# TensorE's row in a scan step: the sum of y two tiles back placed between the two pieces of the next tile's turned product

## The chip, the cores and the metric

The kernel runs on one core of one Trainium2 chip. The metric is device time in microseconds. A core has five engines that run their own instruction rows and meet only through semaphores: TensorE (PE in the profile), VectorE (DVE), ScalarE (ACT), GpSimd (POOL) and SyncE (SP), which issues the transfers. An engine takes its row in order: a wait at one instruction holds everything behind it.

## What is computed

Two images `b` of 1024 tokens with 128 channels go through a block with two residual branches. The first branch is a two-directional Mamba layer, the second a mixture of experts. The costly part is the recurrence of the Mamba layer, for each image and direction:

```python
xc = silu(conv(xh))                     # 256 channels
dbc = xc @ x_proj.T                     # dt, B (16), C (16) per token
delta = softplus(dt @ dt_w.T + dt_b)
def step(h, inp):
    u_t, d_t, B_t, C_t = inp
    h = h * exp(d_t[:, :, None] * A) + (d_t * u_t)[:, :, None] * B_t[:, None, :]
    return (h, einsum('bds,bs->bd', h, C_t))
y = (ys + xc * Dsk) * silu(z)
out = y @ out_proj.T
```

## The kernel before, in words

The loop over `e` runs 128 tiles. A *unit* `u` is one image and direction (4 units of 32 tiles; the second direction scans backwards), and within a unit the tile `t = e % 32` is one of 16 states for one half (128) of the channels. Each tile is 128 channels by 1024 tokens, and passes through four engines:

- ScalarE makes the decay `dA` (L605) and, one block of 128 tokens at a time, scales the input `dBuT`, tokens on partitions, with B (L621).
- TensorE turns `dBuT` into PSUM with channels on partitions, in two pieces of 512 tokens, `dbu_chunk(e + 1, 0)` and `dbu_chunk(e + 1, 1)`, four transposes each, into three banks `dBu0` to `dBu2`. Below they are c0 and c1. A piece waits until the scan three pieces back has freed its bank: in step `e`, c0 waits for both scans of tile `e - 1`, c1 for the first scan of tile `e`.
- VectorE scans the tile in two pieces (L1044 forward, L1047 backward).
- GpSimd multiplies the states by the row of C into `hc` (L519), three buffers deep.
- TensorE turns `hc` back and adds it onto `yT` in PSUM, eight transposes: `y_add(e - 2)`, the sum of y two tiles back, below y(e-2). It waits for that tile's product.

Between these, TensorE's row carries *items*, small pieces of the projections of the next unit and of the end of the last one: kinds X, Z, B, BT, DT, DU for the next unit (X takes two steps, the others one), YT and O for the last unit, and LT, LG and more in the last unit. All items of the loop share one PSUM bank, `pro`. So an item starts only after the item before it has been read out: by ScalarE in its own order (tanh L571 for X and Z, copies for the others) and for X and Z then by VectorE (L920, L924), which does this between the two scans of a tile. So a late item holds the second scan, too.

In steps `t` = 2 and 3 of a unit, TensorE starts `yT` anew with `y_start` (L1260 `yT<-dskip,area`), once VectorE has closed the last unit's half with a gate (L1055). The gate of a half stands on VectorE between the scans of tile `t` = 1 (half 0) or 2 (half 1) and waits for the last y of that half, which TensorE adds in step `t` = 0 or 1.

The four tiles of `DIRECT` (tiles 40, 41 and 72, 73) have their product made by GpSimd (L495), not TensorE: the steps 39, 40, 71 and 72 turn no piece.

The lines L1260 and L1264 are the helpers through which every matmul and transpose go; the tiles' names tell them apart: `dBu<-ident,dBuT` is c0 and c1, `yT<-ident,hc` is a sum of y, `pro<-...` is an item.

Of the kernel before, what the change touches and what calls it, by code (L numbers as in the profile page):

```python
# [138 lines left out]
def build_block(nc, x_d, mod_d, wpack_d, bcast_d, dtw_d, w1_d, w2_d, crow_d, out_d):  # L139
# [5 lines left out]
    with ctx:  # L145
# [188 lines left out]
        def chunks(u):  # L334

            return range(NCH) if u % 2 == 0 else range(NCH - 1, -1, -1)
# [118 lines left out]
        def _(g_):  # L455
# [25 lines left out]
            def pool_du(half, u):  # L481
                _, _, par = unit(u)
                wait_delta(g_, half, u)
                for c in range(NCH):
                    wait_item(g_, "X", half * NCH + c, u)
                g_.tensor_tensor(du[:, half, :], delta[par][:, half, :], xc[par][:, half, :],
                                 ALU.mult).then_inc(du_ready, 1)
# [45 lines left out]
        def _(act):  # L533
# [57 lines left out]
            def softplus(u):  # L591
                _, _, par = unit(u)
                wait_item(act, "DT", NH * NCH - 1, u)
                for half in range(NH):
                    nc.scalar.activation(delta[par][:, half, :], pre[:, half, :], ACT.Softplus).then_inc(delta_ready, 1)  # L595

            def exp_tile(e):

                u, s, half = e // (DS * NH), e // NH % DS, e % NH
                _, dr, par = unit(u)  # L600
                if s == 0:
                    wait_delta(act, half, u)
                if e >= 3:
                    act.wait_ge(scan_done, NCH * (e - 2))
                nc.scalar.activation(dA[:, e % 3, :], delta[par][:, half, :], ACT.Exp,  # L605
                                     scale=Aneg[:, dr, half, s:s + 1]).then_inc(da_ready, 1)
# [651 lines left out]
        def _(pe):  # L1258
# [3 lines left out]
            def turn(out, in_, start, idn=None):  # L1262

                return nc.tensor.matmul(out, in_, ident[:, :] if idn is None else idn, start=start, stop=True,  # L1264
                                        is_transpose=True, skip_group_check=True)
# [139 lines left out]
            def dbu_chunk(e, i):  # L1405

                u, half = e // (DS * NH), e % NH
                g, q = e // NH, NCH * e + i
                c = chunks(u)[i]
                if e == 0 and i == 1:  # L1410
                    pe.wait_ge(high0_ready, 1)
                elif half == 0:
                    pe.wait_ge(dbut_ready, max(NCH * SCALED.index(g) - 1, 0) + i + 1)
                if q >= 3:
                    pe.wait_ge(scan_done, q - 2)
                for k in range(BPC):
                    last = turn(dBu[q % 3][:, k * P:(k + 1) * P],
                                dBuT[:, SCALED.index(g) % 2, c * BPC + k, half * P:(half + 1) * P], True)
                last.then_inc(dbu_ready, 1)

            def y_start(u, half):

                _, dr, par = unit(u)
                if u > 0:
                    pe.wait_ge(gate_done, NH * (u - 1) + half + 1)
                for n in range(NBLK):
                    mm(yT[:, half, n, :], xc[par][:, half, n * P:(n + 1) * P], dskip[:, dr, half, :],
                       n % BPC == 0, True)

            def y_add(e):  # L1430

                half = e % NH
                if e == NT - 1:
                    pe.wait_ge(last_hc, 1)
                else:
                    pe.wait_ge(hc_done, e + 1)
                for n in range(NBLK):
                    last = turn(yT[:, half, n, :], hc[:, e % 3, n * P:(n + 1) * P], False)
                last.then_inc(yacc_done, 1)
# [18 lines left out]
            for e in range(NT):  # L1458
                u, t = divmod(e, DS * NH)
                for i in range(NCH):  # L1460
                    if e + 1 < NT and (e + 1) // NH not in DIRECT:
                        dbu_chunk(e + 1, i)
                for p in PARTS[e]:
                    item_t(*p)
                if t in (2, 3):
                    y_start(u, t - 2)
                if e >= 2:
                    y_add(e - 2)
            def gather(b, ns):

# [174 lines left out]
```

## Time and profile before

| | |
|---|---|
| median of 3 runs | 593.84 us (593.1 to 595.65) |
| the profiled execution's own time | 595.13 us |
| span of its profile | 593.3 us |
| mean granted TensorE clock | 0.945 |
| busy, share of the span | PE 84%, DVE 79%, ACT 74%, POOL 57% |

### The profile page before, as it was taken

To read this page: it belongs to the slowest core of one execution; us is meant where nothing else is said; L and a number is where in the kernel's file an instruction comes from. 1 tells how busy PE (TensorE), PEld (TensorE's weight loads), DVE (VectorE), ACT (ScalarE), POOL (GpSimd) and SP (SyncE) were. 2 spreads that over 40 slices of the span, in tenths; PEclk is the share of its full clock that TensorE was granted. 3 is DMA by queue.
4 is the path that set the end of the run, shared out by engine and by line. 5 is a ranking of instruction groups with operands and counts; after the bars stand their busy time and mean duration, and the time that the engine had idled before them with its cause. 6 is when DMAs were issued, how large, how long until landed. Compare 5 with 4: busy or idle time off the path is not lost.

```text
span 593.3 us, 9187 instructions
## 1 busy us (share of the span) xinstructions
PE 495.7 (84%) x3346; PEld 406.6 (69%) x3346; DVE 465.8 (79%) x709; ACT 439.6 (74%) x835; POOL 339.2 (57%) x159
## 2 busy tenths in 40 slices
PE   3578979996899999698998896788967486999997
PEld 2345856875779677576955676688855375698696
DVE  5856887976988787698899876988999999866422
ACT  2459875999996989999686799987879671374250
POOL 3104655867969777697895767857667573200000
PEclk9988997998999999899999897979989999978999
DMA  8031121221332222123222211312272214000101
GB/s 257 0 115 37 62 81 36 78 78 60 116 107 72 107 72 89 53 81 134 82 72 65 72 76 38 116 67 76 72 215 91 82 42 142 1 1 2 35 1 36
DMA packets 18237, 44.77 MB, mean 75 GB/s; under 512 B 1360, under 2 KB 7632, under 8 KB 17936
## 3 DMA queue, kind: packets, MB, share of 16 engines
q1 hardware_dynamic: 18192, 44.18, 22.3%
q8 instruction: 27, 0.44, 0.3%
q14 instruction: 18, 0.15, 0.1%
HBM read 42.61 MB, written 1.57 MB: 74 GB/s over the span
## 4 chain that ended last, share of the span: by engine, by line
PE 41%; ACT 26%; DVE 23%; issue 7%; POOL 1%; DMA 1%; POOLq 0%; DVEq 0%; ACTq 0%
ACT dBuT L621 12%; PE pro L1260 10%; DVE area L1047 9%; PE yT L1264 9%; PE yT L1260 9%; ACT dA L605 7%; PE dBu L1264 7%; PE dBu L1260 5%; DVE area L1044 3%; PE pro L1264 2%; DVE area L827 1%; ACT th L571 1%; ACT pre L580 1%; DVE pre L1009 1%; ACT area L595 1%
## 5 line engine op out<-in xcount | busy, mean ns | idle before, releaser
L519 POOL TENSOR_TENSOR hc<-area 128x1024 f32<-128x1024 f32 x127 | 302.7, 2389 | 148.1 <-DVE area L1044 87.6
L621 ACT ACTIVATE dBuT<-area,bT 128x256 f32<-128x256 f32 x492 | 208.4, 499 | 8.1 <-PE dBu L1264 8.1
L1264 PE MATMUL dBu<-ident,dBuT 128*128 128x128 f32 x992 | 143.3, 282 | 43.9 <-DVE area L1047 23.5
L605 ACT ACTIVATE dA<-area,Aneg 128x1024 f32<-128x1024 f32 x124 | 141.8, 1144 | 20.3 <-DVE area L1047 13.5
L1264 PEld LDWEIGHTS dBu<-ident,dBuT 128*128 128x128 f32 x992 | 115.1, 145 | 57.5 <-issue 21.2
L1264 PE MATMUL yT<-ident,hc 128*128 128x128 f32 x1024 | 140.7, 283 | 1.7 <-POOL hc L519 1.4
L1264 PEld LDWEIGHTS yT<-ident,hc 128*128 128x128 f32 x1024 | 120.8, 145 | 20.9 <-issue 15.4
L1047 DVE TENSOR_TENSOR_SCAN area<-dA,area,dBu 128x512 f32<-128x512 f32 x62 | 79.2, 1278 | 4.5
L1044 DVE TENSOR_TENSOR_SCAN area<-dA,area,dBu 128x512 f32<-128x512 f32 x62 | 79.2, 1277 | 4.1
L1044 DVE TENSOR_TENSOR_SCAN area<-dA,dBu 128x512 f32<-128x512 f32 x62 | 74.7, 1205 | 9.3 <-PE dBu L1264 8.7
L1047 DVE TENSOR_TENSOR_SCAN area<-dA,dBu 128x512 f32<-128x512 f32 x62 | 74.6, 1204 | 6.0 <-PE dBu L1264 5.5
L1260 PE MATMUL pro<-hT,wtap 128*128 128x512 f32 x96 | 48.2, 627 | 0.2 <-DVE area L924 0.2
L1260 PE MATMUL pro<-wp,hT 128*128 128x256 f32 (+1 forms) x96 | 23.2, 371 | 14.2 <-DVE area L924 12.6
L924 DVE SCALAR_TENSOR_TENSOR area<-th,pro 128x512 f32<-128x512 f32 x16 | 11.0, 687 | 25.4 <-ACT th L571 24.9
L571 ACT ACTIVATE th<-pro 128x512 f32<-128x512 f32 x28 | 16.4, 587 | 15.7 <-PE pro L1260 15.7
L1260 PEld LDWEIGHTS pro<-wp,hT 128*128 128x128 f32 x96 | 15.6, 201 | 18.1 <-DVE area L924 14.6
L1260 PEld LDWEIGHTS pro<-hT,wtap 128*128 128x128 f32 x96 | 17.3, 201 | 13.5 <-issue 12.6
L589 ACT ACTIVATE area<-pro 128x512 f32<-128x512 f32 x14 | 8.3, 591 | 16.9 <-PE pro L1264 16.9
L696 ACT ACTIVATE hc<-dBu,modT 128x512 f32<-128x512 f32 x2 | 1.6, 778 | 25.7 <-PE dBu L1260 25.7
L725 ACT ACTIVATE hc<-yT,wp 128x64 f32<-128x64 f32 x64 | 14.0, 330 | 8.5 <-PE yT L1260 8.5
L1260 PE MATMUL pro<-area,wp 128*96 128x512 f32 x28 | 14.9, 652 | 6.1 <-DVE area L837 6.1
L1260 PE MATMUL yT<-hc,dBuT 128*128 128x64 f32 x128 | 18.0, 302 | 0.0
(235 smaller groups left out, 598.5 us busy)
## 6 DMA issues: line engine op xcount, KB each, us to landing
area<-bc_rows SPq DMA_DIRECT2D x64, 512.0 KB, 3.6
dBuT<-w_in SPq DMA_DIRECT2D x1, 2048.0 KB, 9.1
wp<-wpack_in SPq DMA_DIRECT2D x1, 1030.0 KB, 7.3
x<-x_in SPq DMA_DIRECT2D x2, 512.0 KB, 6.6
hc<-bcast_in SPq DMA_DIRECT2D x1, 1024.0 KB, 10.5
Bb<-bc_rows SPq DMA_DIRECT2D x2, 512.0 KB, 3.9
out<-x SPq DMA_DIRECT2D x4, 256.0 KB, 2.3
bc_rows<-xdbl SPq DMA_DIRECT2D x4, 128.0 KB, 3.8
```

The source lines that it names most:

```text
L519: g_.tensor_tensor(hc[:, e % 3, :], hs[:, e % 3, :], Cb[:, g % 3, :], ALU.mult).then_inc(hc_done, 1)
L571: nc.scalar.activation(th[:, :], src, ACT.Tanh).then_inc(tanh_ready, 1)
L580: nc.scalar.activation(dst[:, half, c * CH:(c + 1) * CH], src, func, bias=dtb(dr, half)).then_inc(item_act, 1)
L589: nc.scalar.activation(yg[:, half, c * CH:(c + 1) * CH], src, ACT.Copy).then_inc(item_act, 1)
L605: nc.scalar.activation(dA[:, e % 3, :], delta[par][:, half, :], ACT.Exp, scale=Aneg[:, dr, half, s:s + 1]).then_inc(da_ready, 1)
L621: return nc.scalar.activation(dBuT[:, SCALED.index(g) % 2, n, :], duT[par][:, n, :], ACT.Copy, scale=bT[:, par, n, s:s + 1])
L725: last = nc.scalar.activation(hid[:, q % 2, i, c, :], up_bank(q)[:, at:at + TOPK], ACT.Gelu_apprx_tanh, bias=b1c[:, 2 * q + i, c:c + 1])
L924: nc.vector.scalar_tensor_tensor(gz[par][:, 2 * j:2 * j + 2, :].rearrange("p n d -> p (n d)"), th[:, :], 1.0, src, ALU.add, ALU.mult).then ...
L1044: nc.vector.tensor_tensor_scan(hs[:, e % 3, lo:hi], decay, inflow, init, ALU.mult, ALU.add).then_inc(scan_done, 1)
L1047: nc.vector.tensor_tensor_scan(hs[:, e % 3, lo:hi][:, ::-1], decay[:, ::-1], inflow[:, ::-1], init, ALU.mult, ALU.add).then_inc(scan_done, 1)
L1260: return nc.tensor.matmul(out, lhsT, rhs, start=start, stop=stop, skip_group_check=True)
L1264: return nc.tensor.matmul(out, in_, ident[:, :] if idn is None else idn, start=start, stop=True, is_transpose=True, skip_group_check=True)
```

## The change

In a step, TensorE's row was c0, c1, items, y. It becomes c0, y, c1, items. In the steps `t` = 2 and 3 nothing moves, since y must follow `y_start` there. In the steps without pieces (before the direct tiles) y now stands ahead of the items. Nothing is added or removed, and no other engine's row changes.

```diff
                 for i in range(NCH):
                     if e + 1 < NT and (e + 1) // NH not in DIRECT:
                         dbu_chunk(e + 1, i)
+                    if i == 0 and e >= 2 and t not in (2, 3):
+                        y_add(e - 2)
                 for p in PARTS[e]:
                     item_t(*p)
                 if t in (2, 3):
                     y_start(u, t - 2)
-                if e >= 2:
                     y_add(e - 2)
```

The first place is TensorE's row in the first unit, from `y_start` of step 3 to the item of step 5. The items here are of kind Z (`pro<-wp,hT`). Before:

```order
L1260 MATMUL yT<-dskip,area1 128x128 x8
L1264 MATMUL yT<-ident,hc 128x128 x8
L1264 MATMUL dBu1<-ident,dBuT 128x128 x4
L1264 MATMUL dBu2<-ident,dBuT 128x128 x4
L1260 MATMUL pro<-wp,hT 128x256 x2
L1264 MATMUL yT<-ident,hc 128x128 x8
L1264 MATMUL dBu0<-ident,dBuT 128x128 x4
L1264 MATMUL dBu1<-ident,dBuT 128x128 x4
L1260 MATMUL pro<-wp,hT 128x256 x2
```

With the change:

```order
L1260 MATMUL yT<-dskip,area1 128x128 x8
L1264 MATMUL yT<-ident,hc 128x128 x8
L1264 MATMUL dBu1<-ident,dBuT 128x128 x4
L1264 MATMUL yT<-ident,hc 128x128 x8
L1264 MATMUL dBu2<-ident,dBuT 128x128 x4
L1260 MATMUL pro<-wp,hT 128x256 x2
L1264 MATMUL dBu0<-ident,dBuT 128x128 x4
L1264 MATMUL yT<-ident,hc 128x128 x8
L1264 MATMUL dBu1<-ident,dBuT 128x128 x4
L1260 MATMUL pro<-wp,hT 128x256 x2
```

The first Z item of the fence has two sums of y between `y_start` and itself, where it had one; from there on there is one y between two items, as before.

The second place is TensorE's row around the direct tiles 40 and 41, from the last O item (its last two rows stand here) to the second half of the X item. Before:

```order
L1264 MATMUL pro<-ident,hT 128x128
L1260 MATMUL pro<-wp,area3 128x128 x2
L1264 MATMUL yT<-ident,hc 128x128 x8
L1260 MATMUL pro<-hT,wtap 128x512 x2
L1264 MATMUL yT<-ident,hc 128x128 x8
L1264 MATMUL dBu0<-ident,dBuT 128x128 x4
L1264 MATMUL dBu1<-ident,dBuT 128x128 x4
L1260 MATMUL pro<-hT,wtap 128x512 x2
```

With the change:

```order
L1264 MATMUL pro<-ident,hT 128x128
L1260 MATMUL pro<-wp,area3 128x128 x2
L1264 MATMUL yT<-ident,hc 128x128 x8
L1260 MATMUL pro<-hT,wtap 128x512 x2
L1264 MATMUL dBu0<-ident,dBuT 128x128 x4
L1264 MATMUL yT<-ident,hc 128x128 x8
L1264 MATMUL dBu1<-ident,dBuT 128x128 x4
L1260 MATMUL pro<-hT,wtap 128x512 x2
```

The sum between the O item and the X item was y(37), and y(38) followed the X item's first half; with the change y(37) stands ahead of this O item, and the sum between O and X is y(38).

The third place is TensorE's row at the start of the last unit, from c0 of tile 97 to `y_start`; the items `pro<-ident,pre` are LT. Before:

```order
L1264 MATMUL dBu2<-ident,dBuT 128x128 x4
L1264 MATMUL dBu0<-ident,dBuT 128x128 x4
L1264 MATMUL pro<-ident,pre 128x128 x4
L1264 MATMUL yT<-ident,hc 128x128 x8
L1264 MATMUL dBu1<-ident,dBuT 128x128 x4
L1264 MATMUL dBu2<-ident,dBuT 128x128 x4
L1264 MATMUL pro<-ident,pre 128x128 x4
L1264 MATMUL yT<-ident,hc 128x128 x8
L1264 MATMUL dBu0<-ident,dBuT 128x128 x4
L1264 MATMUL dBu1<-ident,dBuT 128x128 x4
L1260 MATMUL yT<-dskip,area1 128x128 x8
```

With the change:

```order
L1264 MATMUL dBu2<-ident,dBuT 128x128 x4
L1264 MATMUL yT<-ident,hc 128x128 x8
L1264 MATMUL dBu0<-ident,dBuT 128x128 x4
L1264 MATMUL pro<-ident,pre 128x128 x4
L1264 MATMUL dBu1<-ident,dBuT 128x128 x4
L1264 MATMUL yT<-ident,hc 128x128 x8
L1264 MATMUL dBu2<-ident,dBuT 128x128 x4
L1264 MATMUL pro<-ident,pre 128x128 x4
L1264 MATMUL dBu0<-ident,dBuT 128x128 x4
L1264 MATMUL dBu1<-ident,dBuT 128x128 x4
L1260 MATMUL yT<-dskip,area1 128x128 x8
```

The two sums, y(94) and y(95), for which the gates wait, have moved ahead of c1 and of the LT item of their step.

## Rows read from the trace of the kernel before

**Rows 1.** The page: engines' busy time, and the chain that ended last.

```profile
PE 495.7 (84%) x3346; PEld 406.6 (69%) x3346; DVE 465.8 (79%) x709; ACT 439.6 (74%) x835; POOL 339.2 (57%) x159
...
PE 41%; ACT 26%; DVE 23%; issue 7%; POOL 1%; DMA 1%; POOLq 0%; DVEq 0%; ACTq 0%
```

**Rows 2.** The page's costliest groups: the pieces and the sums of y on TensorE.

```profile
L1264 PE MATMUL dBu<-ident,dBuT 128*128 128x128 f32 x992 | 143.3, 282 | 43.9 <-DVE area L1047 23.5
...
L1264 PE MATMUL yT<-ident,hc 128*128 128x128 f32 x1024 | 140.7, 283 | 1.7 <-POOL hc L519 1.4
```

**Rows 3.** Waits of TensorE, 85 to 485 us: total, times, longest.

```profile
PE dBu L1264 <- DVE area L1047: 22.1, 23, 3.4
PE dBu L1264 <- DVE area L1044: 14.5, 11, 4.6
PE pro L1260 <- DVE area L924: 12.6, 6, 4.8
```

**Rows 4.** Busy time by stretch: length, PE, PEld, DVE, ACT, POOL, clock, DMA.

```profile
171.00:217.00 46.00, 45.71 (x314) 36.21 (x315) 37.17 (x34) 37.56 (x71) 36.52 (x16) 1.00 0.27 93
400.00:485.00 85.00, 63.38 (x509) 56.61 (x508) 79.94 (x119) 68.88 (x131) 58.50 (x26) 0.96 0.32 102
```

**Rows 5.** Timeline, first unit, step 4: TensorE, and ScalarE's tanh.

```profile
66.39 1.04 PE L1264 MATMUL yT<-ident,hc 128*128 128x128 f32 x8
67.26 1.04 PE L1264 MATMUL dBu<-ident,dBuT 128*128 128x128 f32 x8
...
66.90 0.57 ACT L571 ACTIVATE th<-pro 128x512 f32<-128x512 f32 x1
```

**Rows 6.** Timeline, second unit: its start, and the last ScalarE wait before 240 us.

```profile
169.81 0.57 ACT L571 ACTIVATE th<-pro 128x512 f32<-128x512 f32 x1
...
170.56 0.68 DVE L920 SCALAR_TENSOR_TENSOR area<-th,pro 128x512 f32<-128x512 f32 x1
...
171.29 0.66 PE L1264 MATMUL pro<-ident,area 128*128 128x128 f32 x4 [1.04 <-DVE area L920]
...
217.73 0.59 ACT L575 ACTIVATE xdbl<-pro 96x512 f32<-96x512 f32 x1 [0.24 <-PE pro L1260]
```

**Rows 7.** Timeline, direct tiles 40 and 41: TensorE's sums y(37), y(38); GpSimd.

```profile
189.10 1.04 PE L1264 MATMUL yT<-ident,hc 128*128 128x128 f32 x8
...
191.87 1.03 PE L1264 MATMUL yT<-ident,hc 128*128 128x128 f32 x8
...
184.15 4.69 POOL L495 TENSOR_TENSOR dA<-pre,Bb 128x1024 f32<-128x1024 f32 x2
188.79 7.02 POOL L519 TENSOR_TENSOR hc<-area 128x1024 f32<-128x1024 f32 x3
```

**Rows 8.** Timeline, direct tiles 72 and 73: item X, y(70), y(71); GpSimd; VectorE.

```profile
296.92 1.99 PE L1260 MATMUL pro<-hT,wtap 128*128 128x512 f32 x4
298.87 1.09 PE L1264 MATMUL yT<-ident,hc 128*128 128x128 f32 x8
...
303.59 1.09 PE L1264 MATMUL yT<-ident,hc 128*128 128x128 f32 x8
...
296.45 6.99 POOL L519 TENSOR_TENSOR hc<-area 128x1024 f32<-128x1024 f32 x3
...
304.53 0.66 DVE L920 SCALAR_TENSOR_TENSOR area<-th,pro 128x512 f32<-128x512 f32 x1
```

**Rows 9.** Timeline, start of the last unit: c1 of tile 96, y(94), the gate.

```profile
386.93 1.09 PE L1264 MATMUL dBu<-ident,dBuT 128*128 128x128 f32 x4 [4.57 <-DVE area L1044]
...
392.07 1.05 PE L1264 MATMUL yT<-ident,hc 128*128 128x128 f32 x8
...
393.16 1.23 DVE L1055 TENSOR_TENSOR area<-yT,area 128x1024 f32<-128x1024 f32 x1 [1.24 <-PE yT L1264]
```

**Rows 10.** Timeline, ScalarE after the softplus of two units.

```profile
143.02 1.31 ACT L621 ACTIVATE dBuT<-area,bT 128x256 f32<-128x256 f32 x3 [0.26 <-PE dBu L1264]
...
249.58 1.71 ACT L621 ACTIVATE dBuT<-area,bT 128x256 f32<-128x256 f32 x4 [0.28 <-PE dBu L1264]
```

## The prediction

> **What bounds the kernel now.** I read the page first. TensorE is the busiest engine, 84% of the span, but the chain that ended last gives it 41%, ScalarE 26% and VectorE 23% [rows 1]: the bound changes hands. The table of costly groups gives what the change is about. The 992 rows of the pieces stood behind 43.9 us of idle TensorE, most of it waiting for scans; the 1024 rows of the sums of y behind 1.7 us [rows 2]. So TensorE often stands at a piece while a sum that is ready lies behind it. The waits from 85 to 485 us say it again: 22.1 and 14.5 us at pieces for scans, 12.6 us at items for the readout of `pro` [rows 3]. Where does that idle time lie? From 171 to 217 us TensorE is busy 45.71 of 46 us; from 400 to 485 us VectorE is busy 79.94 of 85 and TensorE only 63.38 [rows 4]. So TensorE sets the time of the front of a unit, where it hardly waits, and waits where VectorE, or ScalarE around the softplus, sets the time. Filling idle time in the second kind gives nothing by itself. What counts is what the new order does to three things that others wait for: the items, the gates, the first pieces.
>
> **One sum costs 0.87 us of TensorE's row**: from the start of y at 66.39 to the start of the next piece at 67.26 [rows 5]. The count of transposes is unchanged, so in a saturated stretch the row's length is unchanged. What changes is which sum has been done when an item ends. Before, y(e-3) is done at the end of the item of step e; after, y(e-2). Between two items stand one sum and two pieces in both orders, so a saturated row neither gains nor loses from item to item. The shift is paid once per unit, at t = 4, the first step in which y moves ahead, since two sums then stand between `y_start` and the item. Each item from there is up to 0.87 us later, until TensorE has an idle gap at a piece that swallows the extra sum. Being one sum ahead is of no use to anyone unless somebody waits for a sum or for c0.
>
> **First unit, +0.4.** Item Z of step 4 ended at 66.39, where y began; now at 67.26. ScalarE was not free for its tanh until 66.90 [rows 5], so the lateness that gets through is 67.26 - 66.90 = 0.36 us, say 0.4. Bounds: 0 if a later slack eats it, 0.87 if ScalarE itself is early. ScalarE, the item's next user on VectorE and the second scan all hang on it, so it stays in the chain.
>
> **Second unit, +2.0 and -0.16.** At its start the X item's tanh is not held by TensorE but by ScalarE's own order, ending at 169.81 + 0.57 = 170.38; VectorE read the item at 170.56, behind a gate, and TensorE's next item, 1.04 us idle, followed at 171.29 [rows 6]. An earlier gate therefore gains 170.56 - 170.40 = 0.16 us, no more. From there TensorE is saturated [rows 4] to the handover at 217.73, where ScalarE waits for an item for the last time (0.24 us) [rows 6] and then sets the pace through the softplus. So the 0.87 us of t = 4 come through whole. On top comes the direct place. GpSimd makes two products for tiles 40 and 41 from 184.15 and only then product 38, which ends at 188.79 + 7.02/3 = 191.13 [rows 7]. Before, y(38) began at 191.87, after the X item, and waited for nothing. Now it stands ahead of the X item. The O item ahead of it ended at 189.10, where y(37) began [rows 7]; now, one sum later, at 189.97. TensorE then stands 191.13 - 189.97 = 1.16 us. What is queued behind: half an X item, the pieces of tile 42, the rest of X; VectorE's scans of 42 wait for them. In a saturated stretch nothing gives it back. Sum 0.87 + 1.16 = 2.0, bounds 0.9 (GpSimd early enough) and 3.2 (a whole product of 2.34 us waited for).
>
> **Third unit, +1.6 and -0.16.** Again 0.87 us at t = 4. Product 70 ends at 296.45 + 6.99/3 = 298.78; before, TensorE spent the time until then on the X item, from 296.92, and y(70) followed at 298.87 without loss [rows 8]. Now the X item (1.95 us) stands behind y(70). From y(70) to y(71) took 303.59 - 298.87 = 4.72 us [rows 8], of which about 0.75 was the wait of a piece that now passes beside the moved work; with X and one more sum ahead, the second half of X ends at 298.87 + 3.97 + 1.95 + 0.87 = 305.66, 2.1 us later than 303.59. ScalarE's tanh takes 0.6 us, so VectorE reads it at 306.3 where it did at 304.53 [rows 8]: +1.8 at most. Some of this meets norms on VectorE which end later anyway; I take 1.6, bounds 0.9 and 2.0. VectorE sets the time from here to 333 us and keeps it. The start gives 0.16 as in the second unit.
>
> **Last unit, -1.1.** This is where a sum is waited for. The gate of half 0 stood 1.24 us idle until y(94), begun at 392.07, was done [rows 9]. In the new row y(93) falls into TensorE's 4.57 us of waiting before c1 of tile 96 [rows 9], and y(94) follows c0 of tile 97, ahead of c1 and LT. It is then done by about 391, before VectorE has ended its scan at 391.92 (393.16 less the idle 1.24). So nearly all of 1.24 is gained; I keep 0.1 for the hop: -1.1. ScalarE is well ahead here, and VectorE carries the gain to the end. Bounds 0 and 1.3. The 0.87 us of t = 4 cost nothing where VectorE is the bound [rows 4].
>
> **After each softplus, -0.26 to -0.28, three times.** ScalarE waited 0.26 and 0.28 us for c0 [rows 10], because TensorE had been stuck at an item with y undone. With y done ahead, c0 follows the item at once, and ScalarE, which sets the pace there, gains it: -0.8 in all. Bounds 0 and 0.9.
>
> **The sum.** 0.4 + 2.0 + 1.6 - 0.32 - 1.1 - 0.8 = +1.8 us. Against the profiled execution's own 595.13 us this is 596.9; that execution lies 1.3 us above the median of the runs, so against the median 593.84 it is 595.6 us, 0.3% slower, inside the 0.5% (3 us) that a measurement of this kernel can tell from no change.
>
> **A rule weighed.** The rows show 36.6 us of TensorE waiting at pieces [rows 3] while only 1.7 us stood before sums [rows 2]; the case for a gain is that such time can be filled. The Trainium skill, Perfetto Trace Analysis, Optimization Strategies, says that in general the matmul engine should be kept as highly utilized as possible; by that rule the filled gaps would count as gain, which is the first rival below. The rows of 400 to 485 us speak against it here, with VectorE at 94%.
>
> **Rivals.** *Faster, the idle time is cashed.* For it: 36.6 us is nine times the losses that I count (4.0), and c0 goes to VectorE 0.87 us earlier in every step. Against it: where VectorE waited for c0, c1 comes no earlier, and the items hold the second scan. If one in ten of the waited microseconds came back and the items cost nothing, that and the gains at the starts make -3.7 - 0.3 - 1.1 = -5.1: 588.7 us.
> *Slower, GpSimd's queue.* The same two direct places, deeper: TensorE's late items delay the scans, so GpSimd's three-product tail starts later, and y(38) and y(70) each wait for a whole product, 2.34 us, in place of the 1.16 and about 0.9 counted. With what then follows once more at y(39) and y(71), +2.5 to +3: 598.4 us. It decides once product 38 ends more than 1.2 us later against TensorE's arrival than I have it.
> *Nothing arrives.* ScalarE's and VectorE's own queues eat the late items, the gains being as small: 593.8 us. For it: ScalarE was the later one in the first unit, by 0.5 us.
> *The clock.* With pieces and sums alternating, TensorE might idle for moments at every change of tile, and the grant fall in the saturated stretch, which ran at 1.00 with a change at every 0.4 to 2 us [rows 4]. At 0.94 as over the kernel, 46 us of work in each of three such fronts would be 2.8 us longer, +8 in all: 602 us. The Trainium skill, TensorE: Matmul & The Clock Gate, A second HAM failure mode, tells of a kernel in which cycling through PSUM banks did this. The 1.00 of this stretch does not bear it out.
>
> **Chances.** The forecast, +0.2 to +3.4 us with the bounds above: 0.52, of which 0.05 beyond 3 us. Nothing arrives: 0.12. Slower by GpSimd: 0.19. The clock: 0.02. Faster: 0.15. So faster 0.15, same 0.59, slower 0.26. The likeliest case's own range is 594.0 to 597.4. For 8 in 10 I go down to 591.3, into the faster case, and up to 599.3, above the GpSimd case.
>
> **What would show it.** Right: item Z of step 4 ends about 0.9 us later after `y_start`; TensorE stands 1 us or more at y(38) for L519, and 2 us at y(70), where the wait of sums in all was 1.7 us; the gate at the last unit's start shows no wait for TensorE; c0's wait of ScalarE after the softplus is gone; TensorE's waits at pieces shrink by tens of microseconds with the span unmoved. Wrong: if VectorE's busy share in 171 to 217 us rises, early c0 does speed the front, and I have missed who set it.

## The result: 596.95 us, 0.5% slower

| | before | changed |
|---|---|---|
| median of 11 runs each | 594.21 us (592.62 to 595.65) | 596.95 us (591.7 to 600.07) |
| ratio, 95% interval | | 1.0052 (1.0030 to 1.0074) |
| profiled execution: own time, span | 595.13, 593.3 us | 598.08, 596.4 us |
| mean granted TensorE clock | 0.945 | 0.937 |

The change costs 0.3 to 0.7%, 1.8 to 4.4 us. The ratios here and below leave out single executions more than 1.5% above the fastest of the same kernel: 954.15 us of a2_fronts_old, 602.13 of b2_softplus_only, 598.34 of b4_fronts_old_step10, 598.2 of c1_no_last and 818.77 of the kernel before.

The page of the changed kernel, its engines, the chain that ended last, and the two groups of [rows 1, 2]:

```profile
PE 499.5 (84%) x3346; PEld 410.4 (69%) x3346; DVE 465.5 (78%) x709; ACT 440.2 (74%) x835; POOL 340.4 (57%) x159
...
PE 36%; ACT 26%; DVE 25%; issue 8%; POOL 3%; DMA 1%; POOLq 0%; DVEq 0%; ACTq 0%
...
L1264 PE MATMUL dBu<-ident,dBuT 128*128 128x128 f32 x992 | 157.5, 286 | 39.6 <-DVE area L1047 22.3
...
L1264 PE MATMUL yT<-ident,hc 128*128 128x128 f32 x1024 | 140.7, 283 | 6.6 <-POOL hc L519 6.2
```

The idle time at the pieces went from 43.9 to 39.6 us, that at the sums of y from 1.7 to 6.6: TensorE's wait moved to another instruction. The chain gives TensorE 5 points less and GpSimd 2 more. The waits from 85 to 485 us, against [rows 3]:

```profile
PE dBu L1264 <- DVE area L1047: 19.7, 30, 2.6
PE dBu L1264 <- DVE area L1044: 13.1, 14, 3.7
PE pro L1260 <- DVE area L924: 12.1, 5, 4.6
...
PE yT L1264 <- POOL hc L519: 4.4, 6, 1.9
```

The two stretches of [rows 4] (length, PE, PEld, DVE, ACT, POOL, clock, DMA):

```profile
171.00:217.00 46.00, 44.91 (x307) 36.07 (x306) 33.56 (x31) 34.28 (x64) 34.49 (x15) 0.98 0.21 76
400.00:485.00 85.00, 66.12 (x518) 59.16 (x516) 80.02 (x119) 71.75 (x135) 59.33 (x25) 0.94 0.33 106
```

The *front* of a unit is the part in which TensorE is nearly always busy. VectorE does 33.56 us of work in it where it did 37.17. Part of that is only that the window is fixed and the changed trace runs up to 2 us later in it. Either way the early first pieces don't speed the front up.

**Where the time went.** The tool for this is a plain subtraction: for each tile, the start of its first scan piece in the changed trace minus that in the trace before, tiles counted from 0. A step in this *lateness* is where time is lost or won. The places at which it steps are few:

| from tile to tile | lateness, us | step | what stands there |
|---|---|---|---|
| 5 to 9 | -0.14 to +0.43 | +0.57 | `t` = 4 of the first unit |
| 9 to 22 | +0.43 to -2.32 | -2.75 | TensorE behind a 3 us wait in step 10 |
| 22 to 32 | -2.32 to -2.27 | +0.05 | first softplus |
| 32 to 36 | -2.27 to -0.35 | +1.92 | start of the second unit |
| 36 to 55 | -0.35 to +1.63 | +1.98 | `t` = 4 and tiles 40, 41 |
| 55 to 64 | +1.63 to +2.02 | +0.39 | second softplus |
| 64 to 68 | +2.02 to +1.76 | -0.26 | start of the third unit |
| 68 to 76 | +1.76 to +3.37 | +1.61 | `t` = 4 and tiles 72, 73 |
| 76 to 95 | +3.37 to +2.79 | -0.58 | a stretch at the lower clock, third softplus |
| 95 to 99 | +2.79 to +1.30 | -1.49 | start of the last unit |
| 99 to 127 | +1.30 to +1.13 | -0.17 | last unit |
| 127 to the end | +1.13 to +3.0 | +1.9 | after the loop |

Now the rows at the forecast places. First unit, step 4, timeline; it answers to [rows 5]:

```profile
66.25 1.03 PE L1260 MATMUL pro<-wp,hT 128*128 128x256 f32 x4
...
67.11 0.60 PE L1264 MATMUL dBu<-ident,dBuT 128*128 128x128 f32 x4
67.32 0.60 ACT L571 ACTIVATE th<-pro 128x512 f32<-128x512 f32 x1 [0.47 <-PE pro L1260]
```

The item ends at 67.11, in this trace 0.15 us ahead at its start; so 0.87 us after its old place, the price of one sum. The tanh begins 0.21 us behind it: the handover from TensorE to ScalarE, which the working left out. So 0.57 and not 0.36 us gets through.

The direct tiles 40 and 41 (TensorE, then GpSimd), for [rows 7]:

```profile
190.87 1.09 PE L1264 MATMUL yT<-ident,hc 128*128 128x128 f32 x8 [1.09 <-POOL hc L519]
191.80 1.88 PE L1260 MATMUL pro<-hT,wtap 128*128 128x512 f32 x4
...
188.44 9.36 POOL L519 TENSOR_TENSOR hc<-area 128x1024 f32<-128x1024 f32 x4
```

y(38) stands 1.09 us for the first of four products, which ends at 188.44 + 2.34 = 190.78. The X item stands behind it. Here a wait that the row of before covered with 1.95 us of work is bare.

The direct tiles 72 and 73, for [rows 8]:

```profile
300.62 1.09 PE L1264 MATMUL yT<-ident,hc 128*128 128x128 f32 x8 [1.90 <-POOL hc L519]
301.55 1.88 PE L1260 MATMUL pro<-hT,wtap 128*128 128x512 f32 x4
```

y(70) stands 1.90 us, as forecast. What that wait is worth is another matter, and the shift alone will answer it below.

The start of the last unit, for [rows 9]:

```profile
391.93 1.92 PE L1264 MATMUL yT<-ident,hc 128*128 128x128 f32 x8
...
393.38 1.19 DVE L1047 TENSOR_TENSOR_SCAN area<-dA,dBu 128x512 f32<-128x512 f32 x1
...
394.49 1.20 DVE L1055 TENSOR_TENSOR area<-yT,area 128x1024 f32<-128x1024 f32 x1
```

The gate begins where the scan ends, with no wait shown, although y(94) took 1.92 us, the time of eight transposes at the 1.2 GHz level (1.04 at the 2.4 GHz level).

ScalarE after the softplus of two units, for [rows 10]:

```profile
142.75 0.60 ACT L583 ACTIVATE area<-pro 128x512 f32<-128x512 f32 x1 [0.71 <-PE pro L1264]
...
144.28 1.70 ACT L621 ACTIVATE dBuT<-area,bT 128x256 f32<-128x256 f32 x4
...
249.30 0.60 ACT L571 ACTIVATE th<-pro 128x512 f32<-128x512 f32 x1 [0.26 <-PE pro L1260]
...
253.19 0.60 ACT L571 ACTIVATE th<-pro 128x512 f32<-128x512 f32 x1 [0.66 <-PE pro L1260]
```

ScalarE's wait for c0 is gone. The 0.26 us at 249.30 is no news: the same item cost it 0.25 us before. The waits of 0.71 and 0.66 us for an item that stands behind c0, y and c1 are new. TensorE comes out of a wait of 4.63 us there and runs at the 1.2 GHz level at first:

```profile
137.06 1.11 PE L1264 MATMUL pro<-ident,pre 128*128 128x128 f32 x4 [4.63 <-DVE area L924]
...
139.16 1.91 PE L1264 MATMUL yT<-ident,hc 128*128 128x128 f32 x8
```

How much of the new waits is the order's and how much the clock's, this pair alone can't say; the section on the softplus stretches below compares more traces.

**Two steps that no term foresaw** go with TensorE's clock. At step 10, TensorE before and then changed:

```profile
89.10 1.11 PE L1264 MATMUL dBu<-ident,dBuT 128*128 128x128 f32 x4 [3.10 <-DVE area L1044]
90.00 3.62 PE L1260 MATMUL pro<-hT,wtap 128*128 128x512 f32 x4
93.42 1.88 PE L1264 MATMUL yT<-ident,hc 128*128 128x128 f32 x8
```

```profile
85.39 1.04 PE L1264 MATMUL yT<-ident,hc 128*128 128x128 f32 x8
89.55 0.66 PE L1264 MATMUL dBu<-ident,dBuT 128*128 128x128 f32 x4 [3.12 <-DVE area L1044]
90.12 1.99 PE L1260 MATMUL pro<-hT,wtap 128*128 128x512 f32 x4
```

The wait is equally long, since c1 needs VectorE, which is busy with small arithmetic. Before, the X half behind it took 3.62 us and the sum 1.88; in the changed trace the X half took 1.99. The granted clock of 85 to 100 us was 0.77 against 1.00: behind the wait TensorE ran at the 1.2 GHz level once, and at the 2.4 GHz level the other time. At the start of the second unit it is the other way round. The changed kernel, for [rows 6]:

```profile
166.42 1.09 PE L1264 MATMUL dBu<-ident,dBuT 128*128 128x128 f32 x8
169.30 0.66 PE L1264 MATMUL pro<-ident,area 128*128 128x128 f32 x4 [1.79 <-DVE area L920]
169.79 3.58 PE L1260 MATMUL yT<-dskip,area 128*128 128x128 f32 x16
```

`y_start` took 3.58 us behind a wait of 1.79; before it took 1.95 behind one of 1.04. The new order as such doesn't bring this: a1_direct_old below has the same row here, a wait of 1.07 and a `y_start` of 1.95, and its lateness steps by -0.27 where the changed kernel's steps by +1.92.

### The profile page after: what moved, and what is told of

The parts are those of the page before. It is cut to its first block, busy times and chain, and to the rows that moved or that the text cites. A ratio compares the mean times of both kernels' runs of the same rounds, so it can differ in the third digit from the quotient of the medians.

```text
span 596.4 us, 9187 instructions
## 1 busy us (share of the span) xinstructions
PE 499.5 (84%) x3346; PEld 410.4 (69%) x3346; DVE 465.5 (78%) x709; ACT 440.2 (74%) x835; POOL 340.4 (57%) x159
## 3 DMA queue, kind: packets, MB, share of 16 engines
HBM read 42.61 MB, written 1.57 MB: 74 GB/s over the span
## 4 chain that ended last, share of the span: by engine, by line
PE 36%; ACT 26%; DVE 25%; issue 8%; POOL 3%; DMA 1%; POOLq 0%; DVEq 0%; ACTq 0%
ACT dBuT L621 12%; DVE area L1047 9%; PE yT L1260 9%; PE pro L1260 8%; ACT dA L605 8%; PE yT L1264 7%; PE dBu L1264 6%; DVE area L1044 5%; PE dBu L1260 4%; POOL hc L519 2%; PE pro L1264 2%; DVE area L827 1%; ACT th L571 1%; DVE pre L1009 1%; ACT area L595 1%
## 5 line engine op out<-in xcount | busy, mean ns | idle before, releaser
L1264 PE MATMUL dBu<-ident,dBuT 128*128 128x128 f32 x992 | 157.5, 286 | 39.6 <-DVE area L1047 22.3
L1264 PEld LDWEIGHTS dBu<-ident,dBuT 128*128 128x128 f32 x992 | 117.7, 146 | 72.5 <-issue 37.4
L1260 PE MATMUL pro<-hT,wtap 128*128 128x512 f32 x96 | 46.4, 606 | 0.0
L504 POOL TENSOR_TENSOR rstd<-rstd,mhalf 128x8 f32<-128x8 f32 x4 | 6.6, 1645 | 21.7 <-DVE rstd L1002 21.5
```

What stands on the lines that cost most here:

```text
L504: g_.tensor_tensor(rstd[:, rs], rstd[:, rs], mhalf[:, rs], ALU.pow).then_inc(rstd_ready, 1)
L1260: return nc.tensor.matmul(out, lhsT, rhs, start=start, stop=stop, skip_group_check=True)
```

## The experiments

**Theory (order):** the kernel's time moves by what the table shows at the places of the forecast, and each place can be bought or left out by itself. **Rival (clock):** the sizes at the places are right or not, but what a median shows is set by which stretches run at the lower clock, after the loop above all.

All twelve kernels have one form. Where the condition holds, y(e-2) stands ahead of c1; elsewhere it stands behind the items, as before:

```diff
+                early = t not in (2, 3) and (CONDITION)
                 for i in range(NCH):
                     if e + 1 < NT and (e + 1) // NH not in DIRECT:
                         dbu_chunk(e + 1, i)
-                    if i == 0 and e >= 2 and t not in (2, 3):
+                    if i == 0 and e >= 2 and early:
                         y_add(e - 2)
                 for p in PARTS[e]:
                     item_t(*p)
                 if t in (2, 3):
                     y_start(u, t - 2)
+                if e >= 2 and not early:
                     y_add(e - 2)
```

Each ratio is to the kernel before on the same chip, whose median was 594.0 to 594.4 us. It is formed without the executions named above, which the medians include, and is not the quotient of two medians.

| kernel | median us | ratio, 95% interval |
|---|---|---|
| a1_direct_old | 597.7 | 1.0076 (1.0042 to 1.0109) |
| a2_fronts_old | 590.13 | 0.9928 (0.9905 to 0.9952) |
| a3_fronts_only | 597.64 | 1.0076 (1.0048 to 1.0105) |
| a4_step10_only | 591.49 | 0.9975 (0.9947 to 1.0002) |
| b1_last_unit | 595.03 | 1.0031 (1.0004 to 1.0058) |
| b2_softplus_only | 590.79 | 0.9952 (0.9927 to 0.9977) |
| b3_shift_only | 593.75 | 1.0022 (0.9988 to 1.0055) |
| b4_fronts_old_step10 | 588.53 | 0.9895 (0.9855 to 0.9935) |
| c1_no_last | 590.38 | 0.9958 (0.9934 to 0.9983) |
| c2_no_last_step10 | 589.31 | 0.9932 (0.9907 to 0.9958) |
| c3_starts_t0 | 586.38 | 0.9897 (0.9860 to 0.9934) |
| c4_softplus_step10 | 589.27 | 0.9935 (0.9906 to 0.9964) |

### The direct places undone

```diff
+                early = t not in (2, 3) and (e not in (39, 40, 71, 72))
```

> The changed order everywhere except in the steps 39, 40, 71 and 72 around the direct tiles, where y stands behind the items again. Theory A (the items wait for GpSimd there): the profile of the changed kernel gained 1.1 us of lateness in the second unit's scans there and 0.7 in the third's, so this kernel is 1.8 us faster than the changed one: +0.9 us against the kernel before, and sums of y wait for L519 under 3 us in all instead of 6.2. Theory B (the loss is TensorE's clock at the units' starts and in the tail): no gain here, +2.7 us.

It was no faster: 1.0076 (some 4.5 us), above both values expected, with an interval that overlaps the changed kernel's. TensorE at 40 and 41:

```profile
185.51 0.33 PE L1264 MATMUL pro<-ident,hT 128*128 128x128 f32 x1 [0.78 <-DVE acc L982]
...
188.73 1.99 PE L1260 MATMUL pro<-hT,wtap 128*128 128x512 f32 x4
190.56 1.03 PE L1264 MATMUL yT<-ident,hc 128*128 128x128 f32 x8
...
191.87 1.04 PE L1264 MATMUL yT<-ident,hc 128*128 128x128 f32 x8
```

The wait for GpSimd is gone, and so is its profit. Going back to the old order leaves no sum between the two O items, and the second then waits 0.78 us for the first one's readout. Going forward again puts two sums (190.56 and 191.87) between the halves of X. The lateness still rises from -2.18 (tile 36) to -0.44 (tile 45), by 1.74 where the changed kernel has 1.98. The shift is paid at each entry into the new order, not once per unit.

### All fronts in the old order, and the fronts alone

```diff
+                early = t not in (2, 3) and (u == 3 or t < 2 or t > 21)
```

> The changed order only in tiles t = 0, 1 and 22 to 31 of the first three units and in the whole last unit; the old order in the fronts, t = 4 to 21. Theory A (the fronts lose, the gate and the softplus gain): none of the 0.4 + 2.0 + 1.5 us is lost and about 1.1 + 0.8 + 0.3 is gained: -2.2 us, 592.0. Theory B (the clock at the second unit's start loses 1.6 us in any kernel that has y(31) done before the idle time there): -0.6 us.

```diff
+                early = t not in (2, 3) and (u < 3 and 3 < t < 22)
```

> The complement: the changed order only in t = 4 to 21 of the first three units. Theory A (order alone): +0.4 +2.0 +1.5 = +3.9 us. Theory B (in the first unit the sum that fills the idle time at 85 us keeps TensorE at the full clock and gives 2.8 us): +1.1 us, with TensorE's clock at 1.00 from 90 to 96 us.

These split the change in two, and the signs are those of the order theory: the fronts alone cost 0.76% (4.5 us, forecast 3.9), the rest alone gains 0.72% (4.3 us, forecast 2.2). The two don't add up, though: +4.5 and -4.3 make +0.2, and the whole change measured +3.1 us. What the rest gains beyond its forecast isn't explained by its order; its only trace is that of the execution of 954.15 us, which can't be compared tile by tile. In the trace of a3_fronts_only the lateness steps by +0.58 in the first unit (tiles 5 to 9), from -1.61 to +0.40 in the second (+2.01) and from +0.94 to +2.54 in the third (+1.60), each within 0.03 us of the changed kernel's.

### Step 10 alone

```diff
+                early = t not in (2, 3) and (e == 10)
```

> One single sum of y moved, y(8) in step 10, into the 3.3 us in which TensorE waits for a scan behind VectorE's gate arithmetic. Order alone: the row behind the wait is one sum shorter, -0.9 us at most. Clock theory: TensorE stays at 2.4 GHz behind the wait, the X items there run in 1.8 instead of 3.4 us, -2.8 to -3.5 us: 591.0.

The median says -0.25% with an interval that touches 1. Here the trace tells more than the time. The same two places, `y_add` early or late, appear in all the traces, with three outcomes of the clock. I read the lateness from tile 9 to 20:

| clock of 85 to 100 us | y(8) late, as before | y(8) early, step 10 only |
|---|---|---|
| 0.77 | 0 and -0.1 (before, c1) | not seen |
| 0.89 | -1.06 (b3) | -1.95 (a4) |
| 1.00 | -2.76, -2.75 (b1, b2) | -3.47, -3.45, -3.47, -3.47 (b4, c2, c3, c4) |

So y(8) in the 3 us wait is worth 0.7 to 0.9 us by order, and the clock behind the wait up to 2.8 us. The row of b1_last_unit is there the same as before's, and yet:

```profile
88.56 0.66 PE L1264 MATMUL dBu<-ident,dBuT 128*128 128x128 f32 x4 [3.11 <-DVE area L1044]
89.14 1.98 PE L1260 MATMUL pro<-hT,wtap 128*128 128x512 f32 x4
```

The new place does not decide the clock. With y(8) late it was 0.77, 0.77, 0.89, 1.00, 1.00 in five traces; with y(8) early 0.89 in three and 1.00 in five, never 0.77. That is too few to call the odds different. In the changed kernel the order's 0.7 is not kept: its lateness goes to -3.18 and comes back to -2.32 at tile 21, by the 0.87 of the shift, which the wait had swallowed for ten tiles only. The total, -2.75, is that of the clock alone.

### The last unit alone, the softplus stretches alone

```diff
+                early = t not in (2, 3) and (u == 3)
```

> The changed order in the last unit alone. Theory A (the gate of the last unit's start no longer waits for y(94)): -1.1 to -1.5 us and nothing else, VectorE's gate without a wait. Rival (VectorE is the bound there whatever TensorE does): 0.

```diff
+                early = t not in (2, 3) and (u < 3 and t > 21)
```

> The changed order only in t = 22 to 31 of the first three units. Order alone: ScalarE no longer waits 0.26 and 0.28 us for the first piece, -0.8 us in all. Clock theory: TensorE's sum is done ahead of the 4.8 us in which it stands at an item, so it comes out of it with less to do, at the same lower clock: no more than -1 us.

In b1_last_unit the lateness steps from -3.65 (tile 95) to -4.85 (tile 99): -1.2, as the order theory has it. In time the kernel missed its expectation of -1.1 to -1.5 us: it came out 0.31% slower. Its trace leaves the loop 4.6 us ahead, 2.8 of them from step 10, and yet ends 2.6 us behind. The stretch after the loop, 498 to 540 us, in before, b1_last_unit and b4_fronts_old_step10:

```profile
498.00:540.00 42.00, 39.02 (x250) 33.67 (x251) 29.09 (x113) 21.63 (x58) 3.30 (x2) 0.88 0.03 12
```

```profile
498.00:540.00 42.00, 40.47 (x232) 35.39 (x232) 26.56 (x112) 19.57 (x55) 3.30 (x2) 0.77 0.00 1
```

```profile
498.00:540.00 42.00, 38.15 (x291) 32.73 (x290) 30.86 (x136) 21.32 (x60) 3.31 (x2) 1.00 0.01 2
```

The code there is the same in all three. At 0.77 TensorE gets 232 matmuls done in 42 us, at 1.00 it gets 291. Here the rival has it.

b2_softplus_only gained 0.48% (2.9 us), but its own trace steps by -0.01 at the first softplus and +0.44 at the second, much as the changed kernel's. With all the traces side by side the softplus step sorts by the granted clock of the stretch (120 to 150 us, 240 to 269 us):

| | clock 0.94 | clock 0.88 or 0.89 |
|---|---|---|
| first softplus, y late | 0, -0.13, -0.11 (before, a3, b3) | +0.06, +0.91 (a4, b1) |
| first softplus, y ahead | -0.22 to -0.23 (a1, b4, c1 to c4) | +0.05, -0.01 (changed, b2) |
| second softplus, y late | 0, +0.12 (before, a4) | +0.54 to +0.82 (a3, b1, b3) |
| second softplus, y ahead | -0.18 to -0.30 (b4, c1 to c4) | +0.39 to +0.53 (changed, a1, b2) |

In each column the new order is ahead of the old, mostly by 0.1 to 0.4 us; at the second softplus the lower clock costs 0.5 to 0.8 us in either order. a1_direct_old, with the new order in nearly all of the front, has no wait of ScalarE at the first softplus:

```profile
139.79 1.53 PE L1264 MATMUL yT<-ident,hc 128*128 128x128 f32 x8
...
142.57 0.58 ACT L583 ACTIVATE area<-pro 128x512 f32<-128x512 f32 x1
```

TensorE's granted clock over the 8 us from 137 was 0.79 here and 0.66 in the changed kernel, whose ScalarE waited the 0.71 us shown above. b2_softplus_only, with the old order in its fronts, waits 0.66 us at the same place. So the wait goes with the clock and not with items made late by the front. Some 0.6 us (three times 0.2) of b2's 2.9 are then the order's, and the rest is not shown to be.

### The shift alone

```diff
+                early = t not in (2, 3) and (u in (1, 2) and 3 < t < 7)
```

> The changed order only in t = 4 to 6 of the second and third unit: the shift of one sum ahead of the items is paid, the wait for GpSimd at the direct tiles is not, since y stands behind the items again from step 39 and 71 on. Shift theory: +0.9 us of lateness in each of the two units' scans where TensorE sets the time, 1.1 to 1.8 us in all. Rival (the whole loss of the fronts is the wait for GpSimd): 0.

The time can't tell 1 us from nothing here (1.0022, 0.9988 to 1.0055); the trace can. It has +0.87 us in the second unit (+0.57 to +1.44) and no more. In the third, though, the whole +1.57 (+2.26 to +3.83), although y(70) stands behind X here as before. So the third unit's second part is not what the forecast said. What is it? VectorE and GpSimd in the trace before:

```profile
302.80 0.68 DVE L1002 TENSOR_SCALAR rstd<-mv 128x8 f32<-128x8 f32 x1
...
301.11 4.68 POOL L519 TENSOR_TENSOR hc<-area 128x1024 f32<-128x1024 f32 x2
```

and in that of b3_shift_only:

```profile
305.93 2.10 DVE L1002 TENSOR_SCALAR rstd<-mv 128x8 f32<-128x8 f32 x1
...
303.33 4.67 POOL L519 TENSOR_TENSOR hc<-area 128x1024 f32<-128x1024 f32 x2
```

An instruction on 8 values per partition takes 0.68 us once and 2.10 us the other time. It ends at 303.48 where GpSimd's product of the moment ends at 301.11 + 2.34 = 303.45, and at 308.03 where the second product of the row ends at 303.33 + 4.67 = 308.00. VectorE's instruction lasts until GpSimd has ended its product. It does so both times that it runs beside a product in each of thirteen traces: 26 times it ends within 0.04 us of a product's end, having taken 0.66 to 2.13 us. With GpSimd idle the same instruction takes 0.17 us:

```profile
508.73 0.17 DVE L1002 TENSOR_SCALAR rstd<-mv 128x8 f32<-128x8 f32 x1
```

With the shift L1002 starts 3.13 us later, the product only 2.22, so it just misses a boundary (305.67) and pays a whole further product. The changed kernel has the same, `L1002` from 305.43 for 2.12 us with a product ending at 307.53. The lateness of its scans goes from +2.62 to +4.07 there, and 0.70 us is given back two tiles on. The Trainium skill, SBUF — State Buffer, Who interferes with whom, says that VectorE and GpSimd share one port pair as an exclusive lock; the ends of these two rows agree.

### All fronts old, with step 10

```diff
+                early = t not in (2, 3) and (u == 3 or t < 2 or t > 21 or e == 10)
```

> The kernel with the old order in the fronts (median 590.1) with y(8) of step 10 moved ahead as well. If the two gains add: -4.3 us from the first and -1.5 to -2.7 from the second, 587 to 588.5. If both are one and the same matter of TensorE's clock: 590.

1.05% faster than before (0.65 to 1.45%): it beats both kernels. It takes the gains of the softplus stretches, of step 10 and of the last unit, and leaves the full fronts alone. It rests on six executions, from 584.56 to 598.34 us; with the longest counted, their mean lies 0.75% below that of the kernel before. c3_starts_t0 below bears it out with seven.

### Is it the last unit or the clock after it?

```diff
+                early = t not in (2, 3) and (u < 3 and (t < 2 or t > 21))
```

> The sum moves ahead only in the steps t = 0, 1 and t > 21 of the first three units; the last unit keeps the old order, so its gate stands 1.2 us idle for TensorE again. It is a2_fronts_old without the last unit. Order theory (the moved sums add up, each where it stands): it loses the gate's 1.2 us against a2_fronts_old, which measured -0.72%, so -0.5%, about 591.1 us, with the gate showing a wait for TensorE of about 1.2 us. Clock theory (the last unit's new order costs more in the tail after 495 us, by a lower granted clock there, than the gate gives, as b1_last_unit with +0.3% suggests): -0.9% or better, with the granted clock of 498 to 540 us at 0.88 or above.

```diff
+                early = t not in (2, 3) and (u < 3 and (t < 2 or t > 21) or e == 10)
```

> c1_no_last plus the sum y(8) ahead in step 10. If step 10 gives its own 0.3% wherever it stands (b4_fronts_old_step10 against a2_fronts_old), it is 0.3% below c1_no_last. Against b4_fronts_old_step10 (-1.05%) order theory says 1.2 us more, -0.85%; clock theory says -1.1% or better.

```diff
+                early = t not in (2, 3) and (u == 3 or t == 0 or t > 21 or e == 10)
```

> As b4_fronts_old_step10, but in step t = 1 of each of the first three units the old order (y(31), y(63) behind the YT item). It tells whether the pause ahead of the YT item and y_start, 1.8 us in the changed kernel, comes from the sum of step t = 1 having been done early. If so: granted clock of 166 to 176 us is 1.00, and y_start takes 1.8 us. The first gate, that of half 0 at t = 1, is still early; that of half 1 at t = 2 waits for TensorE as before. Order theory: the same time as b4_fronts_old_step10 within 0.2%, at most 0.3 us slower by the gates.

```diff
+                early = t not in (2, 3) and (u < 3 and t > 21 or e == 10)
```

> b2_softplus_only (-0.48%) plus y(8) ahead in step 10; no unit start and no last unit. If the parts add, -0.5 - 0.3 = -0.8%, about 589.5 us. If the clock's outcome at step 10 is drawn anew from run to run whatever the row there (in the profile of b2_softplus_only the wait of step 10 already ended 2.8 to 3.3 us earlier than before, with the same row), it adds nothing: -0.5%.

Without the last unit, a2's -0.72% becomes -0.42%, and b4's -1.05% becomes -0.68%: both times the last unit's new order gains 0.3 to 0.4%, about 2 us. So the clock theory of a last unit that costs more than it gives falls, and what made b1_last_unit slower is best put down to the clock after the loop, as its trace has it. The intervals are 0.2 to 0.4% wide to each side, so each pair alone is weak. The traces agree in the sign and have a smaller size. From tile 95 to 99 b4 and c3 step by -1.50, but c1 and c2, with the old order in the last unit, step by -0.63 and -0.68 as well. Their gate waits less than before:

```profile
388.83 1.22 DVE L1055 TENSOR_TENSOR area<-yT,area 128x1024 f32<-128x1024 f32 x1 [0.76 <-PE yT L1264]
```

It stood 1.24 us before. The sum y(93), in step 95 of the third unit, is already done ahead of TensorE's long wait in c1, so the row behind that wait is shorter. The last unit's own part is then 0.8 to 0.9 us here, and 1.2 in b1, which leaves y(93) where it was.

c2 against c1 and c4 against b2 give step 10 another 0.26% and 0.17%, each inside its error, in line with 0.7 us (0.12%) by order. c4 thus lies between the two values expected of it (-0.5 and -0.8%), and c2, at 2.2 us behind b4 where 1.2 was expected, can't be told from either theory.

c1_no_last shows the small places with the clock of before up to the third unit: -0.23 at the first softplus, -0.26 at the second unit's start, -0.18 at the second softplus, -0.23 at the third unit's start. The last one is shown to be the order's: all kernels with the new starts have -0.23 to -0.26 there, all others 0 to +0.01. That at the second unit's start isn't: c4_softplus_step10, which moves nothing there, steps by -0.26 too, and a3, a4 and b3 by about 0.

c3_starts_t0 gives -1.03%, the same as b4. `y_start` took 1.95 us, behind a wait of 1.07. But b4 has y(31) early and a wait of 1.08 as well, so the sum of `t` = 1 is not what made the wait 1.79 in the changed kernel.

## Why the prediction was right, and where not

The forecast was +0.3%, the result +0.52% (0.30 to 0.74), inside the range and at the upper end of the likeliest case's own. The working by its steps:

- **One sum costs 0.87 us, and between two items stands one sum in both orders: shown.** The step of 0.87 appears in b3's second unit to the hundredth. "Paid once per unit" holds only while the order isn't left: a1 paid it twice.
- **First unit +0.4: 0.57.** The handover of 0.21 us was left out.
- **Second unit +2.0: 1.98 (2.01 in a3), shown**, 0.87 without the direct place (b3), with the wait for GpSimd at 1.09 for 1.16.
- **Third unit +1.6: 1.61, right by coincidence.** 0.87 is the shift. The rest was put down to X standing behind y(70), where TensorE did stand 1.90 us. But b3 and a1, which leave y(70) behind X, step by 1.57 and 1.61 too. It is the 1.4 us that L1002 waits for GpSimd, less 0.70 given back. "Some of this meets norms on VectorE" had the engine right, and the sign wrong: the norm is the cost.
- **Last unit -1.1: -1.49, and -1.20 where nothing else moved (b1).** Shown; some of the -1.49 is y(93), as c1 has it.
- **The starts, -0.16 each.** In the third unit -0.26, shown. In the second unit no run shows it, and in this pair the +1.92 of the place hides it.
- **After each softplus -0.8 in all: not seen in this pair, and yet about right by order.** The steps were +0.05 and +0.39, and the third can't be told from the clock. At equal clock the new order is ahead by some 0.2 us (the table above), with ScalarE's wait for c0 gone as forecast. What ate it is that TensorE stayed longer at the lower clock behind its wait of 4.6 us (0.66 against 0.79 over 8 us), so that ScalarE waited 0.71 and 0.66 us for items. The working had no term for that.

What does the order make in all? The steps that other traces bear out are 0.57 + 1.98 + 1.61 - 0.26 - 1.49 - 0.17 = +2.24 us. With 0.2 for each of the three softplus stretches it is +1.6, my estimate, where the forecast had +1.8. The remaining +1.4 of the +3.0 us between the two traces are steps that other kernels with the same rows do not have: -2.75 at step 10, +1.92 at the start of the second unit, +1.9 after the loop, and the losses at the softplus. They are large and cancel in part. So the forecast of the order is right in sign and size, in the third unit by coincidence. That the time landed at +0.5% and not elsewhere in the range is in part luck, since the clock moves the same program by more than the whole effect. The rival *the clock* was priced for the fronts, which ran at 0.98 to 1.00; it acts behind long waits and after the loop.

*The idle time is cashed* fell: VectorE's share of the front did not rise, and the time did not fall. "Waits at pieces shrink by tens of microseconds" was wrong by its own logic. TensorE's work is the same, so its idle time (593.3 - 495.7 = 97.6 us before, 596.4 - 499.5 = 96.9 now) can only move.

The question behind it, whether filling TensorE's waits pays, has an answer by place. It does where something downstream waits for the sum or for the row (the gates, the softplus, step 10), and the kernels that fill only these are 1% faster than before, about half of it by order. It costs where the row is full. In the changed kernel the costs outweigh the gains.

**Open:** of b4's and c3's 6 us, the steps by order explain about 3 (0.7 at step 10, 0.6 at the softplus, 0.2 at the third unit's start, 1.5 at the last unit). The rest goes with a higher mean granted clock, in nearly all runs of both (0.956 to 0.965, one run of b4 at 0.934) against 0.940 to 0.951 for before. Whether and why the place of a few sums favours that clock was not found. Nor was why the fronts alone and the rest alone don't add up to the change.

## What to carry to other kernels

Moving a block ahead in an in-order row is paid by the first thing behind it at every entry into the new order; so move it only at the places where a wait ahead of it is long and somebody waits for the block, and leave the full stretches alone. Subtract two traces tile by tile and read the steps before believing a median: of the four largest steps here, three go with the clock. When an instruction far from the edit changes its duration, look at which product of the neighbouring engine it ends with.

## What the runs showed of the hardware

- The same program comes out at different clocks: 30 runs of the kernel before went from 589.26 to 595.78 us. Six lay at 589.3 to 589.8 with a mean granted clock of 0.951, and twelve at 593.3 to 594.5 with 0.942. Behind the same 3.1 us wait TensorE ran at the 1.2 GHz level in some traces and at the 2.4 GHz level in others (granted clock of 85 to 100 us: 0.77 to 1.00). The Trainium skill, TensorE: Matmul & The Clock Gate, HAM oscillation — how this bites in real kernels, tells of waits that let the clock fall; here the place agrees, and the outcome varies.
- A `y_start` cost 3.58 us behind a wait of 1.79, and 1.95 us behind waits of 1.04 to 1.08. Steps of +1.63 appear in the first unit of a4 (lateness +0.03 to +1.66) and of b3 (+0.09 to +1.72), where no instruction has moved: `y_start` took 3.49 and 3.39 us there, behind an item that had waited 2.29 and 2.30 us in place of 0.97.
- Transposes alone bring TensorE to the 2.4 GHz level: in the changed kernel it did nothing but 128x128 fp32 transposes from 137.06 us on, and eight of them took 1.91 us at 139.16 and 1.04 us at 142.99.
- VectorE's `tensor_scalar` on 128x8 took 0.17 us with GpSimd idle. Beside GpSimd's products of 2.34 us it took 0.66 to 2.13 us and ended with a product 26 times out of 26. The wait stands inside the instruction's duration, with no idle time and no releaser shown, and its price depends on the phase.
